# Layer 1 attention with queries and keys in two float32r parts, 34-row packs in both 64-row halves of the array, shared by scores and maximum pass

## Chip, cores and metric

One core of a Trainium2 chip. The metric is the time of one execution of the whole program on the device, in microseconds. The program computes two transformer layers over 2 x 1,024 tokens of width 128; the change lies in the attention of layer 1.

## What is computed

Layer 1's attention, cut to its core (16 heads of width 8, S = 1,024, scores softmaxed without a causal mask, with a decay that depends on the distance of two tokens):

```python
q = x @ W_q
latent_kv = (x @ W_k + x @ W_v) @ W_down_kv          # 32 wide
k_rec = (latent_kv @ W_up_k).reshape(b, s, H, HD).transpose(0, 2, 1, 3)
v_rec = (latent_kv @ W_up_v).reshape(b, s, H, HD).transpose(0, 2, 1, 3)
scores = einsum('bhqd,bhkd->bhqk', qh, k_rec) / sqrt(d) * exp(-0.01 * abs(t[:, None] - t[None, :]))
attn = softmax(scores, axis=-1)
out = einsum('bhqk,bhkd->bhqd', attn, v_rec)
x = layernorm(x + out.reshape(b, s, d) @ W_o)
```

Before it stand layer 0's attention and experts, behind it a normalisation, layer 1's experts and the last layer norm.

## The kernel before

The decay is a product of a growing and a falling exponential on either side of the diagonal, so queries and keys exist in two variants ("var" 0 and 1). `project_l1` works through four groups of 512 tokens. PE multiplies by the weights in float32, VectorE multiplies the result by a decay (line 1011, 4 products a group: two variants of q and of k), ScalarE rounds to bfloat16 (first part), VectorE subtracts (1016), ScalarE rounds again (second part, 967), POOL (two of the last on VectorE, 1001) forms the third part. Parts are stored to DRAM (`q_parts`, `k_parts`). The values, with a column of ones per head, are made by PE at line 928 and copied to `a_V` by VectorE (996).

`attention_l1` works in 8 turns of 4 heads (`NIT`), each in two halves of 512 queries (`NHALF` = 16). A half has 9 groups (`NT`), 144 in all. A group is one key block against 512 queries, in four units, one a head; where the diagonal cuts it, a unit has two matmuls, one for each variant. Group g on PE: scores of three units into a ring of three banks (1317: 74 rows, nine products of parts and two rows that carry minus the query's maximum), then the maximum pass for a later half (1286), the fourth unit, then the weighing of group g-2 (`weigh`, 1336: four heads side by side in four column strips, two passes each). ScalarE takes the exponential of each unit (1373), POOL clears the wrong side of the diagonal in some groups (1260), ScalarE copies a finished half from OUT (1363).

The maximum pass makes for each of 128 queries and one head all 1,024 scores from bfloat16 packs of their own (`MaxPacks`, tiles QM and KM, 32 rows, four row strips of the array) into two slots `mring`; VectorE multiplies by a correction and reduces (1385, one instruction a tile). There are 16 tiles a half, 256 in all; `LEAD` = 22 run before the first group, `issued(g)` says how many are due by group g (one or two a group). When the 16 tiles of a half are read, VectorE negates the maxima and splits them, PE turns them (`turn`, 1295), VectorE copies them (1406), and SP writes them as rows 72 and 73 of the query pack (`max_rows`, 1205).

Each engine runs its program in the order in which it is written. SP's queue carries the pack loads (QP 1180, KP 1192, QM 1084, KM 1094 and 1097), the stores of the outputs, and in halves 1 to 3 the stores of the second batch's parts. Packs are double-buffered by turn. PE waits for them at `scores` with T = 0 and at `max_tile` with i = 0.

## Time and profile before

| | us |
|---|---|
| median of 3 runs | 1570.79 (1562.11 to 1572.23) |
| the profiled execution | 1561.7 |
| its span, first to last instruction | 1559.6 |
| busy: PE, VectorE, ScalarE, POOL | 1334.3, 1128.4, 906.1, 474.1 |
| PE loading weights | 751.4 |
| mean granted clock of TensorE | 0.917 |

Engines: PE is TensorE (PEld its weight loads, which overlap matmuls), DVE VectorE, ACT ScalarE, POOL GpSimd, SP the DMA queue. A duration of a matmul in the rows includes its way through the array, so that neighbours overlap: how far their starts lie apart is the time that one costs. A row with "x3" merges three neighbours, its duration runs from the first start to the last end. PEclk is the granted clock, 1.00 for 2.4 GHz and 0.50 for 1.2. Names in rows leave out digits: `a_QP` is `a1_QP0` or `a1_QP1`.

### The profile page before, as it was taken

The numbers are of one execution on the slowest core, as the hardware profiler recorded it, in microseconds if no ns is written. First come the engines' busy times: TensorE is split into PE (matmuls) and PEld (weight loads), VectorE is DVE, ScalarE is ACT, GpSimd is POOL, SyncE is SP. The second block draws the span as 40 slices with busy tenths as digits, with TensorE's granted clock in tenths as the row PEclk, the third lists the DMA queues.
The fourth block names the chain that finished last, engine by engine and source line by source line (L and its number), as shares of the span: only waits on it lengthen the run. The fifth ranks groups of instructions, "written<-read, shape, count | busy, mean of one in ns | idle before, by whom it ended". The sixth has DMA issues, their size and how long they took to land. (4 is left out here: it accounts for less than half of the span.)

```text
span 1559.6 us, 23543 instructions
## 1 busy us (share of the span) xinstructions
PE 1334.3 (86%) x7952; PEld 751.4 (48%) x7952; DVE 1128.4 (72%) x1737; ACT 906.1 (58%) x1496; POOL 474.1 (30%) x986
## 2 busy tenths in 40 slices
PE   4298988619999999999754989999999979999998
PEld 1133333407877778777321222222222225777776
DVE  4366674377999999998547766888888243778885
ACT  3288885105555555555330766787887802767774
POOL 3255453003343343343220233223442301212210
PEclk8599999859999999999855898999999968999999
DMA  5524420015666666663347556665563040022110
GB/s 139 107 56 88 80 61 8 3 41 127 151 150 147 151 155 140 157 148 72 123 96 92 72 128 123 102 106 87 88 98 49 15 157 3 26 97 82 61 49 27
DMA packets 71415, 142.57 MB, mean 91 GB/s; under 512 B 11815, under 2 KB 44648, under 8 KB 64392
## 3 DMA queue, kind: packets, MB, share of 16 engines
q1 hardware_dynamic: 70660, 140.62, 41.3%
q8 instruction: 59, 0.97, 0.3%
q10 hardware_dynamic: 648, 0.59, 0.1%
q14 instruction: 48, 0.39, 0.1%
HBM read 124.20 MB, written 16.71 MB: 90 GB/s over the span
## 5 line engine op out<-in xcount | busy, mean ns | idle before, releaser
L1385 DVE CUSTOM_DVE_ANT_0 a_junk<-a_mring,a_COR 128x1024 bf16<-128x1024 f32 x256 | 304.8, 1222 | 90.0 <-PE a_mring L1286 89.8
L1373 ACT ACTIVATE a_PR<-a_ring 128x512 f32<-128x512 f32 x576 | 300.7, 603 | 118.7 <-PE a_ring L1317 118.6
L1260 POOL TENSOR_SCALAR_AFFINE_SELECT a_PR<-a_PR 128x128 f32<-128x128 f32 x512 | 134.6, 293 | 304.0 <-ACT a_PR L1373 303.8
L803 ACT ACTIVATE e_HH<-e_H 128x512 fp32r<-128x512 f32 x184 | 116.4, 633 | 162.5 <-DVE e_H L851 161.8
L1317 PE MATMUL a_ring<-a_QP,a_KP 74*128 74x512 bf16 (+3 forms) x768 | 181.2, 341 | 13.1 <-issue 5.7
L402 DVE TENSOR_SCALAR a_PR<-a_PR,a_lo,a_hi 128x1024 f32<-128x1024 f32 (+1 forms) x160 | 122.1, 774 | 77.1 <-ACT a_PR L376 74.4
L376 ACT ACTIVATE a_PR<-a_ring,a_ng 128x1024 f32<-128x1024 f32 (+1 forms) x160 | 155.0, 1033 | 13.3 <-PE a_ring L305 12.5
L1336 PE MATMUL a_OUT<-a_PR,a_V 128*9 128x512 f32 (+3 forms) x1536 | 154.7, 500 | 0.0
L822 DVE TENSOR_TENSOR e_HL<-e_H,e_HH 128x512 fp32r<-128x512 f32 x138 | 140.3, 1017 | 13.2
L1317 PEld LDWEIGHTS a_ring<-a_QP,a_KP 74*128 74x128 bf16 x768 | 57.9, 99 | 172.4 <-ACT a_PR L1373 119.6
L1676 DVE TENSOR_TENSOR e_HL<-e_GL,e_HH 128x512 fp32r<-128x512 f32 x144 | 109.2, 763 | 37.6 <-ACT e_HH L1644 34.1
L745 POOL TENSOR_TENSOR e_HL<-e_H,e_HH 128x512 fp32r<-128x512 f32 x46 | 78.8, 1712 | 181.1 <-ACT e_HH L803 181.1
L278 POOL TENSOR_SCALAR_AFFINE_SELECT a_PR<-a_PR 128x128 f32<-128x128 f32 x256 | 98.5, 410 | 110.6 <-DVE a_PR L402 110.6
L1637 ACT ACTIVATE e_GL<-e_psF,e_BF 128x512 f32<-128x512 f32 x144 | 99.2, 690 | 53.4 <-PE e_psF L1595 52.9
L851 DVE TENSOR_TENSOR e_H<-e_T,e_ROUTE 128x512 f32<-128x512 f32 x176 | 122.9, 698 | 1.5
L845 DVE TENSOR_TENSOR e_T<-e_SG,e_psU 128x512 f32<-128x512 f32 x176 | 119.4, 679 | 1.3 <-PE e_psU L761 1.1
L796 ACT ACTIVATE e_SG<-e_psG 128x512 f32<-128x512 f32 x184 | 108.6, 590 | 17.2 <-PE e_psG L761 17.0
L1286 PE MATMUL a_mring<-a_KM,a_QM 32*128 32x512 bf16 (+3 forms) x704 | 82.9, 349 | 36.0 <-DVE a_top L1385 21.9
L325 PE MATMUL a_OUT<-a_PR,a_V 128*32 128x256 f32 (+1 forms) x1280 | 87.5, 367 | 10.3 <-DVE OALL L407 10.3
L305 PE MATMUL a_ring<-a_QP,a_KP 128*128 128x512 bf16 (+3 forms) x384 | 88.3, 333 | 8.4 <-ACT a_PR L376 8.4
L759 PE MATMUL e_psG<-e_XH,e_WH 128*128 128x512 f32 x184 | 72.5, 394 | 8.6 <-POOL e_WL L740 8.6
L770 PE MATMUL e_acc<-e_HH,e_WH 128*128 128x512 f32 x184 | 76.5, 416 | 3.0 <-POOL e_HL L745 2.8
(232 smaller groups left out, 2344.8 us busy)
## 6 DMA issues: line engine op xcount, KB each, us to landing
e_ROUTE<-routing SPq DMA_DIRECT2D x24, 704.0 KB
a_QP<-q_parts SPq DMA_DIRECT2D x72, 192.0 KB
e_RAW<-in_w_chunks SPq DMA_DIRECT2D x46, 192.0 KB, 7.5
a_QM<-q_parts SPq DMA_DIRECT2D x64, 128.0 KB, 5.4
e_GATE<-gates SPq DMA_DIRECT2D x8, 1024.0 KB, 4.7
e_ROUTE<-routing SPq DMA_DIRECT2D x8, 640.0 KB
a_KP<-k_parts SPq DMA_DIRECT2D x24, 192.0 KB
e_ROUTE<-routing SPq DMA_DIRECT2D x8, 576.0 KB
```

The costliest lines, as they stand in the source:

```text
L376: nc.scalar.activation(PR[T][:, j, 0:WIDTH0[T]], ring[n % RING][:, 0:WIDTH0[T]], ACT.Exp, scale=ng[:, head]).then_inc(ring_read, 1)
L402: nc.vector.tensor_scalar(p, p, lo[:, head], hi[:, head], ALU.max, ALU.min).then_inc(clamped, 1)
L803: nc.scalar.activation(HH[n % NH][:], HT[n % NH][:], ACT.Copy).then_inc(high_done, 1)
L822: nc.vector.tensor_tensor(HL[n % NH][:], HT[n % NH][:], HH[n % NH][:].bitcast(F32), ALU.subtract)\
L845: nc.vector.tensor_tensor(T[n % 2][:], SG[n % 2][:], psU[n % 2][:], ALU.mult).then_inc(mul_done, 1)
L851: nc.vector.tensor_tensor(HT[n % NH][:], T[n % 2][:], ROUTE[c % NW][:, grp(g)], ALU.mult).then_inc(h_ready, 1)
L1260: last = nc.gpsimd.affine_select(out=d, in_=d, compare_op=keep, fill=0.0, base=0, pattern=[[step, P]], channel_multiplier=-step)
L1317: last = nc.tensor.matmul(ring[n % NRING][:, a - h % 2 * GW:b - h % 2 * GW], KP[s][:, j, var, kb * P:(kb + 1) * P], QP[s][:, h % 2, j, var ...
L1336: last = nc.tensor.matmul(OUT[j * HP:j * HP + VC, a:b], V[:, b0 + kb, v0:v0 + VC], PR[g % NPR][:, j, a:b], start=(T == 0), stop=(T == NT - ...
L1373: nc.scalar.activation(PR[g % NPR][:, j, :], ring[n % NRING][:], ACT.Exp).then_inc(s_read, 1)
L1385: nc.vector.tensor_tensor_reduce(out=junk[:, i % 2, :], in0=mring[k % 2][:], in1=COR[:, c:c + S], scale=1.0, scalar=-3.0e38, op0=ALU.mult, ...
L1676: nc.vector.tensor_tensor(HL[n % NH][:], GL[n % 4][:], HH[n % NH][:].bitcast(F32), ALU.subtract).then_inc(low_done, 1)
```

## The change

Queries and keys are kept in two float32r parts instead of three bfloat16 ones. ScalarE rounds once, VectorE subtracts straight into the second part. A pack has 34 rows: four products of parts (32) and the two maximum rows. Heads 0 and 1 of a turn lie in partitions 0 to 33, heads 2 and 3 in 64 to 97. The same packs serve the maximum pass; while it reads a pack, the two rows of the queries must be zero, so POOL clears them (`clear`) and the maxima are written afterwards. The maximum order alternates between the halves of the array (2, 0, 3, 1), and PE alternates pieces of scores in one half with pieces of a maximum tile in the other (`group`). The value products move from the projection to the start of `attention_l1`, their copies to ScalarE. Between the leading maximum tiles stand matmuls whose results nothing uses (`keep_busy`). Stores of heads 4 to 15 of the first batch are issued by ScalarE, those of the second batch in halves 1 to 4 by SP.

The core of the diff follows; of the lines taken away only a few stand, since the functions before are printed above.

```diff
+PARTS1 = 2
...
+        W, parts, first_stored = t["W"], packs.parts, t["first_stored"]
+        DEC = t["PR"][:, 0:2].rearrange("p r j c -> p (r j c)").rearrange("p (w n) -> p w n", w=NV)
+        lat = t["PR"][0:DL + 1, 2].rearrange("p j c -> p (j c)")
+        loaded, dec_loaded = t["loaded"], t["dec_loaded"]
+        kv = sb("p1_kv", [P, TOK], F32)
+        val = sb("p1_val", [P, NV, 2, GW], F32)
...
+                            packs.store(sp, g, w, i, 0, HQ, first_stored)
                 sp.wait_ge(first_stored, 2 * NV * 2 * 16)
...
+                packs.load_q(sp, 0)
+                packs.load_q(sp, 1)
...
+                def high(g, w):
                     act.wait_ge(val_done, g * NV + w + 1)
...
+                    nc.scalar.activation(parts[:, w, 0, grp(g)], val[:, w, g % 2], ACT.Copy).then_inc(high_done, 1)
...
+                act.wait_ge(first_stored, 2 * NV * 2 * 16)
+                packs.load_k(act, 0)
...
+                            dve.wait_ge(high_done, g * NV + w)
+                            nc.vector.tensor_tensor(parts[:, w - 1, 1, grp(g)], val[:, w - 1, g % 2], parts[:, w - 1, 0, grp(g)].bitcast(F32),
+                                                    ALU.subtract).then_inc(low_done, 1)
...
+                nc.gpsimd.memset(lat[DL:DL + 1, :], 1.0).then_inc(rows_set, 1)
+                pool.wait_ge(rows_set, 1)
+                n = 1
+                for h in range(2):
+                    packs.clear(h, rows_set)
+                    pool.wait_ge(rows_set, n + 2)
+                    packs.set_ones(h, rows_set)
+                    pool.wait_ge(rows_set, n + 4)
+                    n += 4
...
-MAX_ORDER = (0, 2, 1, 3)
+HROWS = 64
+NROWS = 2 * PARTS1 * HD
+MAX_ORDER = (2, 0, 3, 1)
...
+class Packs:
+    Q_LOADS, K_LOADS = 2 * 2 * 16, 2 * 3 * 16
     def __init__(self, nc, ctx, QS, KS):
         sb, sem = sbuf(nc, ctx), Sems(nc, ctx)
...
+        self.nc, self.QS, self.KS = nc, QS, KS
+        self.parts = sb("p1_parts", [P, 4, PARTS1, TOK], F32R)
+        self.Q = [sb(f"a1_QP{s}", [HROWS + NROWS + 2, 2, 2, 2, GW], F32R) for s in range(2)]
+        self.K = [sb(f"a1_KP{s}", [HROWS + NROWS + 2, 2, 2, S], F32R) for s in range(2)]
+        self.q_loaded = [[sem(f"q_loaded{s}{half}") for half in range(2)] for s in range(2)]
+        self.k_loaded = [sem(f"k_loaded{s}") for s in range(2)]
+    def store(self, eng, g, w, i, h0, h1, done):
+        tok = slice(g * GW, (g + 1) * GW)
+        eng.dma_start((self.QS if w < 2 else self.KS)[h0:h1, w % 2, i, :, tok], self.parts[h0 * HD:h1 * HD, w, i, tok].bitcast(F32))\
+            .then_inc(done, 16)
+    def load_q(self, eng, h):
+        it, half = h // 2, h % 2
         b, q, s = it // NQUAD, it % NQUAD, it % 2
...
+        tok = slice(b * S + half * GW, b * S + (half + 1) * GW)
+        for pair in range(2):
+            heads = slice(q * HQ + pair * 2, q * HQ + pair * 2 + 2)
             for r in range(2):
...
+                rows = slice(pair * HROWS + r * 16, pair * HROWS + r * 16 + 16)
+                eng.dma_start(self.Q[s][rows, half].rearrange("r h a t -> r (h a) t").bitcast(F32),
+                              self.QS[heads, :, :, :, tok].rearrange("h a i d t -> (i d) (h a) t")).then_inc(self.q_loaded[s][half], 16)
     def load_k(self, eng, it):
         b, q, s = it // NQUAD, it % NQUAD, it % 2
...
+        tok = slice(b * S, (b + 1) * S)
+        for pair in range(2):
+            heads = slice(q * HQ + pair * 2, q * HQ + pair * 2 + 2)
+            r0 = pair * HROWS
+            for rows, i0, i1 in ((slice(r0, r0 + 16), 0, 2), (slice(r0 + 16, r0 + 24), 1, 2), (slice(r0 + 24, r0 + 32), 0, 1)):
+                eng.dma_start(self.K[s][rows].rearrange("r h a t -> r (h a) t").bitcast(F32),
+                              self.KS[heads, :, i0:i1, :, tok].rearrange("h a i d t -> (i d) (h a) t")).then_inc(self.k_loaded[s], 16)
+    def clear(self, h, done):
+        for pair in range(2):
+            rows = slice(pair * HROWS + NROWS, pair * HROWS + NROWS + 2)
+            self.nc.gpsimd.memset(self.Q[h // 2 % 2][rows, h % 2].rearrange("r h a t -> r (h a t)").bitcast(F32), 0.0).then_inc(done, 1)
...
+    def max_head(m):
+        return MAX_ORDER[m % HQ]
+    def unit_head(g, n):
+        first = issued(g - 1) if g else LEAD
+        swap = first < issued(g) and max_head(first) < 2
+        return (2, 3, 0, 1)[n] if swap else n
...
+                    sp.dma_start(OD[h // 2, :, h % 2 * GW:(h % 2 + 1) * GW], OST[h % 2][:]).then_inc(out_stored[h % 2], 16)
                 max_rows(0)
...
+                sp.wait_ge(stored[0], STORES * 16)
+                packs.load_q(sp, 2)
+                packs.load_k(sp, 1)
+                packs.load_q(sp, 3)
                 for h in range(NHALF):
                     it = h // 2
+                    if h % 2 == 0 and 1 <= it < NIT - 1:
+                        sp.wait_ge(s_read, h * UNITS)
+                        packs.load_k(sp, it + 1)
+                        packs.load_q(sp, h + 3)
+                    if h % 2 == 1 and it + 2 < NIT:
+                        sp.wait_ge(s_read, h * UNITS)
+                        if it + 2 == NQUAD:
+                            sp.wait_ge(stored[1], STORES * 16)
+                        packs.load_q(sp, h + 3)
                     if h:
                         store(h - 1)
...
+                    if h + 1 < NHALF:
                         max_rows(h + 1)
...
+                    if LATE_FROM <= h < LATE_FROM + STORES // LATE_EACH:
+                        for n in range((h - LATE_FROM) * LATE_EACH, (h - LATE_FROM + 1) * LATE_EACH):
+                            packs.store(sp, 2 + n // 8, n % 4, n // 4 % 2, 0, H, stored[1])
...
+                def clear(h):
+                    packs.clear(h, cleared)
+                    pool.wait_ge(cleared, (h - 1) * 2)
+                for h in (2, 3):
+                    clear(h)
                 for g in range(NGROUP):
...
+                    T, h = g % NT, g // NT
+                    half = h % 2
+                    if 1 <= h < NHALF - 3 and T == (1 if half else KB // 2 + 1):
+                        pool.wait_ge(s_read, h * UNITS)
+                        pool.wait_ge(masked, masked_groups(g - 1) * HQ)
+                        clear(h + 3)
...
+                    s, row, j = h // 2 % 2, i // HQ, max_head(m)
+                    rows = slice(j // 2 * HROWS, j // 2 * HROWS + NROWS + 2)
+                    if a == 0:
+                        if i == 0:
+                            pe.wait_ge(packs.q_loaded[s][h % 2], (h // 4 + 1) * packs.Q_LOADS)
+                            pe.wait_ge(packs.k_loaded[s], (h // 4 + 1) * packs.K_LOADS)
+                            if h >= 2:
+                                pe.wait_ge(cleared, (h - 1) * 2)
+                        slot_free(k)
+                    last = nc.tensor.matmul(mring[k % 2][:, a:b], QP[s][rows, h % 2, j % 2, var, row * P:(row + 1) * P],
+                                            KP[s][rows, j % 2, var, a:b], start=True, stop=True)
+                    if b == S:
+                        last.then_inc(m_filled, 1)
+                def score_piece(g, n, a, b, kb, var):
+                    h, T, u, j = g // NT, g % NT, g * HQ + n, unit_head(g, n)
+                    s, a, b = h // 2 % 2, a - h % 2 * GW, b - h % 2 * GW
+                    rows = slice(j // 2 * HROWS, j // 2 * HROWS + NROWS + 2)
+                    if a == 0:
+                        if T == 0 and n == 0:
+                            pe.wait_ge(m_rows, (h + 1) * 64)
+                        if u >= NRING:
+                            pe.wait_ge(s_read, u - NRING + 1)
+                    last = nc.tensor.matmul(ring[u % NRING][:, a:b], KP[s][rows, j % 2, var, kb * P:(kb + 1) * P],
+                                            QP[s][rows, h % 2, j % 2, var, a:b], start=True, stop=True)
+                    if b == GW:
+                        last.then_inc(s_filled, 1)
                 def turn(h):
                     k = turn_slots[h]
                     pe.wait_ge(neg_done, 3 * (h + 1))
                     slot_free(k)
                     for part in range(2):
...
+                        last = nc.tensor.transpose(mring[k % 2][0:2 * NTILE, part * GW:part * GW + P], neg_part[:, part, :].bitcast(F32),
+                                                   consts["ident"][:])
                     last.then_inc(m_filled, 1)
...
+                def group(g):
                     for h in range(1, NHALF):
                         if turn_group(h) == g:
                             turn(h)
...
+                    tiles = range(issued(g - 1) if g else LEAD, issued(g))
+                    parts_of_unit = list(segments(g % NT, g // NT % 2))
+                    for two in range(2):
+                        scores = [(n, *piece) for n in (2 * two, 2 * two + 1) for piece in parts_of_unit]
+                        maxima = max_pieces(tiles[two]) if two < len(tiles) else []
+                        for x in range(max(len(scores), len(maxima))):
+                            if x < len(scores):
+                                score_piece(g, *scores[x])
+                            if x < len(maxima):
+                                max_piece(tiles[two], *maxima[x])
...
+                def values(f):
+                    if f >= NRING:
+                        pe.wait_ge(v_kept, f - NRING + 1)
+                    for n in range(f * FILL, min(f * FILL + FILL, B * KB)):
+                        last = nc.tensor.matmul(ring[f % NRING][:, n % FILL * VW:(n % FILL + 1) * VW], lat[:, n * P:(n + 1) * P], WV[:],
+                                                start=True, stop=True)
+                    last.then_inc(v_ready, 1)
+                def keep_busy(n):
+                    nc.tensor.matmul(ring[n % NRING][:], ID[:], ID[:].unsqueeze(1).to_broadcast([P, GW // P, P]), start=True, stop=True)
+                for f in range(NFILL):
+                    values(f)
                 pe.wait_ge(cor_loaded, 32)
...
                 for m in range(LEAD):
                     if m == tiles_until_turn(0):
                         turn(0)
...
+                    for piece in max_pieces(m):
+                        max_piece(m, *piece)
+                    if m == 0:
+                        pe.wait_ge(v_kept, NFILL)
+                    for n in range(2):
+                        keep_busy(n)
+                for n in range(12):
+                    keep_busy(n)
+                pe.wait_ge(out_clear, 1)
                 for g in range(NGROUP + LAG):
                     if g < NGROUP:
...
+                        group(g)
...
+                for f in range(NFILL):
+                    keep_values(f)
+                for n in range(STORES):
+                    packs.store(act, n // 8, n % 4, n // 4 % 2, HQ, H, stored[0])
```

PE in the main loop, one group of an odd half with two maximum tiles. Before, from one weighing (`a_OUT`) to the next, scores in `a_ring`, maxima in `a_mring`:

```order
2403 L1336 MATMUL a_OUT<-a_PR,a_V 9x512 x4
2404 L1317 MATMUL a_ring<-a_QP,a_KP 128x512 x3
2405 L1286 MATMUL a_mring<-a_KM,a_QM 128x384
2406 L1286 MATMUL a_mring<-a_KM,a_QM 128x128
2407 L1286 MATMUL a_mring<-a_KM,a_QM 128x512
2408 L1286 MATMUL a_mring<-a_KM,a_QM 128x384
2409 L1286 MATMUL a_mring<-a_KM,a_QM 128x128
2410 L1286 MATMUL a_mring<-a_KM,a_QM 128x512
2411 L1317 MATMUL a_ring<-a_QP,a_KP 128x512
```

After, a group of the same kind, scores and maxima by turns:

```order
2497 L1302 MATMUL a_OUT<-a_PR,a_V 9x512 x4
2498 L1259 MATMUL a_ring<-a_QP,a_KP 128x512
2499 L1244 MATMUL a_mring<-a_KP,a_QP 128x384
2500 L1259 MATMUL a_ring<-a_QP,a_KP 128x512
2501 L1244 MATMUL a_mring<-a_KP,a_QP 128x128
2502 L1244 MATMUL a_mring<-a_KP,a_QP 128x512
2503 L1259 MATMUL a_ring<-a_QP,a_KP 128x512
2504 L1244 MATMUL a_mring<-a_KP,a_QP 128x384
2505 L1259 MATMUL a_ring<-a_QP,a_KP 128x512
2506 L1244 MATMUL a_mring<-a_KP,a_QP 128x128
2507 L1244 MATMUL a_mring<-a_KP,a_QP 128x512
```

Three scores, maxima, one score have become pairs in which a score's matmul and a maximum's stand side by side. The group that holds the turn, after:

```order
2548 L1302 MATMUL a_OUT<-a_PR,a_V 9x512 x4
2549 L1269 MATMUL a_mring<-ident,a_neg_part 32x128 x2
2550 L1259 MATMUL a_ring<-a_QP,a_KP 128x256
2551 L1244 MATMUL a_mring<-a_KP,a_QP 128x512
2552 L1259 MATMUL a_ring<-a_QP,a_KP 128x256
2553 L1244 MATMUL a_mring<-a_KP,a_QP 128x128
```

Before, the turn (L1295) stood behind three units of scores; now it is ahead of all, and the first maximum piece follows one score piece. SP's queue after, from the start of a turn to the next one's first loads (`q_parts` and `k_parts` to packs, `a_MT` the maximum rows):

```order
299 L1051 DMA a_KP<-k_parts 16x4x1024
300 L1051 DMA a_KP<-k_parts 8x4x1024 x2
301 L1051 DMA a_KP<-k_parts 16x4x1024
302 L1051 DMA a_KP<-k_parts 8x4x1024 x2
303 L1040 DMA a_QP<-q_parts 16x4x512 x4
304 L1163 DMA o_sums<-a_OST 128x512
305 L1157 DMA a_QP<-a_MT 1x16x128 x4
306 L1040 DMA a_QP<-q_parts 16x4x512 x4
```

Before, a turn had six loads of QP, five of KP, eight of QM and twelve of KM; now it has eight of QP and six of KP.

## Rows read from the trace of the kernel before

**Rows 1.** Windows by stage: range, length, busy us (instructions), clock, DMA share, GB/s.
```profile
759.00:814.00 55.00, 34.42 (x72) 14.65 (x72) 28.60 (x42) 22.84 (x40) 19.70 (x15) 0.67 0.37 86
814.00:826.00 12.00, 0.00 (x0) 0.00 (x0) 0.53 (x2) 1.28 (x1) 0.00 (x0) 0.50 0.79 89
826.00:852.00 26.00, 12.54 (x64) 2.71 (x64) 24.18 (x45) 0.00 (x0) 0.00 (x0) 0.50 0.76 99
852.00:870.00 18.00, 18.00 (x106) 5.22 (x104) 12.55 (x22) 11.18 (x22) 8.45 (x32) 0.59 0.08 22
904.00:911.00 7.00, 1.36 (x3) 0.28 (x3) 0.00 (x0) 0.74 (x2) 0.37 (x2) 0.75 0.76 229
960.00:968.00 8.00, 5.92 (x37) 1.75 (x38) 2.38 (x4) 3.22 (x7) 1.55 (x6) 0.64 0.24 72
1043.00:1210.00 167.00, 160.55 (x1338) 47.70 (x1334) 137.95 (x253) 134.78 (x259) 61.41 (x234) 1.00 0.51 83
```

**Rows 2.** Groups by line: operation and count | busy us, mean ns | idle before, releaser.
```profile
L1385 DVE CUSTOM_DVE_ANT_0 a_junk<-a_mring,a_COR 128x1024 bf16<-128x1024 f32 x256 | 304.8, 1222 | 90.0 <-PE a_mring L1286 89.8
L1286 PE MATMUL a_mring<-a_KM,a_QM 32*128 32x512 bf16 (+3 forms) x704 | 82.9, 349 | 36.0 <-DVE a_top L1385 21.9 <-DMA a_KP<-in_ones 12.9
```

**Rows 3.** Timeline of PE, one group of the loop: start, duration, instructions.
```profile
1083.28 0.82 PE L1317 MATMUL a_ring<-a_QP,a_KP 74*128 74x512 bf16 x3
1084.03 0.39 PE L1286 MATMUL a_mring<-a_KM,a_QM 32*128 32x256 bf16 x3
1084.36 0.39 PE L1317 MATMUL a_ring<-a_QP,a_KP 74*128 74x512 bf16 x1
1084.68 1.04 PE L1336 MATMUL a_OUT<-a_PR,a_V 128*9 128x512 f32 x8
1085.65 0.60 PE L1317 MATMUL a_ring<-a_QP,a_KP 74*128 74x512 bf16 x2
```

**Rows 4.** Timeline of PE, the group that holds the turn.
```profile
1077.05 0.82 PE L1317 MATMUL a_ring<-a_QP,a_KP 74*128 74x512 bf16 x3
...
1078.79 0.58 PE L1286 MATMUL a_mring<-a_KM,a_QM 32*128 32x128 bf16 x6 [0.70 <-DVE a_top L1385]
...
1080.60 0.60 PE L1317 MATMUL a_ring<-a_QP,a_KP 74*128 74x512 bf16 x2
```

**Rows 5.** Timeline of ScalarE, copies of finished halves out of OUT.
```profile
885.31 0.60 ACT L1363 ACTIVATE a_OST<-a_OUT 128x512 f32<-128x512 f32 x1 [0.41 <-PE a_OUT L1336]
...
1043.23 0.60 ACT L1363 ACTIVATE a_OST<-a_OUT 128x512 f32<-128x512 f32 x1 [0.41 <-PE a_OUT L1336]
...
1067.15 0.60 ACT L1363 ACTIVATE a_OST<-a_OUT 128x512 f32<-128x512 f32 x1 [0.41 <-PE a_OUT L1336]
...
1232.47 0.60 ACT L1363 ACTIVATE a_OST<-a_OUT 128x512 f32<-128x512 f32 x1
...
1251.05 0.60 ACT L1363 ACTIVATE a_OST<-a_OUT 128x512 f32<-128x512 f32 x1 [1.75 <-PE a_OUT L1336]
```

**Rows 6.** Float32r matmuls of layer 0's experts, and weight loads by type.
```profile
600.40 0.39 PE L761 MATMUL e_psG<-e_XH,e_WL 128*128 128x512 f32 x1
600.63 0.39 PE L759 MATMUL e_psU<-e_XH,e_WH 128*128 128x512 f32 x1
...
L761 PEld LDWEIGHTS e_psG<-e_XH,e_WL 128*128 128x128 f32 x184 | 34.8, 189 | 7.5
L1317 PEld LDWEIGHTS a_ring<-a_QP,a_KP 74*128 74x128 bf16 x768 | 57.9, 99 | 172.4 <-ACT a_PR L1373 119.6 <-issue 33.6 <-DMA a_KP<-k_parts 3.4
...
751.80 0.97 PEld L496 LDWEIGHTS n0m_scale<-mean_of,n0m_Q 128*128 128x128 f32 x8 [0.26 <-ACT n0m_Q L533]
```

**Rows 7.** The projection: VectorE's product, and PE's passes in order of time.
```profile
L1011 DVE TENSOR_TENSOR p_val<-p_psQ,p_DEC 128x512 f32<-128x512 f32 x8 | 5.1, 678 | 3.5 <-PE p_psQ L920 3.5
...
760.10 1.02 PE L917 MATMUL p_psKV<-X,p_wv 128*128 128x512 f32 x2
760.96 1.02 PE L920 MATMUL p_psQ<-X,p_wq 128*128 128x512 f32 x2
```

297 lines of the change are left out of this document (65 added, 232 removed).

## The prediction

> **What bounds the kernel now.** The change touches one stretch, layer 1's projection and attention, so I read the windows by stage first. The projection takes 759 to 814 us, then come 12 us in which no compute engine does anything, 26 us in which only the maximum pass runs ahead, and the main loop from 852 to 1251 [rows 1]. In the undisturbed part (1043 to 1210, the last row) PE is busy 160.6 of 167 us at full clock, VectorE 138.0, ScalarE 134.8. The reader should see that PE sets the pace there and that the next two bounds lie close together.
>
> The copies out of OUT mark the halves: 1043.23 to 1067.15 is 23.9 us per half of nine groups, 2.66 us a group; the last one, which has no maxima beside it, takes 18.6 (1232.47 to 1251.05) [rows 5]. Scaled to one half, VectorE is busy 23.9 x 138.0/167 = 19.7 us and ScalarE 23.9 x 134.8/167 = 19.3: however fast PE becomes, a half with maxima costs about 19.7.
>
> Inside one group [rows 3] PE does: three scores from 1083.28, maxima at 1084.03, one score at 1084.36, the weighing at 1084.68, next group at 1085.65, in all 2.37 us. Two scores stand 0.215 apart ((0.82 - 0.39)/2), so three end their streams at 1083.93, yet the maxima start 0.10 later; the same 0.10 stands at each of the four changes between the 74-row, 32-row and 9-column shapes. The sum is 4 x 0.215 + 0.23 (maxima, in four row strips at once) + 0.87 (weighing: 0.97 less one gap) + 4 x 0.10 = 2.36. A second tile in a group adds 0.3. That is where the change works. The Trainium skill (TensorEngine Tiling, Key Properties) says that a change of tiling mode drains the engine; the trace agrees with 0.10 us.
>
> **Part 1, the loop on PE.** Removed: two of four shape changes a group (-0.20), and the maxima's own slot (-0.23, or -0.5 with two tiles), since a maximum tile runs in the 64-row half that the scores do not use. Each half of the array then has 1,024 columns per pair of scores, 2,048 a group. In float32r a 512-column matmul steps at 0.23 (600.40 to 600.63), scores and pairs 4 x 0.2275 = 0.91 [rows 6].
>
> Added: the weight loads. A float32r load lasts 189 ns where the 74-row bf16 one lasts 99, and eight float32 loads in a row take 0.97, (0.97 - 0.19)/7 = 0.111 each [rows 6]. Each of 768 + 704 = 1,472 pieces has one: 10.2 a group, 1.13 us if one port serves both halves, which is more than the 0.91 of streaming. Two bounds for one group, PE in program order (the ten pieces of the two-tile group whose rows stand above: 512/384/512/128/512, then the same with the halves of the array swapped), a load allowed once the piece before it in its half has started:
> - one port for both halves: starts at 0.11, 0.22, 0.34, 0.44, 0.56, 0.78, 0.78, 1.01, 1.01, 1.12, end 1.35;
> - a port each: 0.11, 0.11, 0.34, 0.34, 0.45, 0.68, 0.68, 0.90, 0.90, 1.02, end 1.24.
>
> Worked through in the same way, the groups of the loop average 1.39 and 1.15: split scores cost most with one port (14 loads), and a long score holds the short maximum piece behind it. With 0.87 weighing and 2 x 0.09 for changes: 2.43 or 2.20 a group, 21.9 or 19.8 a half. Then the turn: before, it and VectorE's lateness (0.70 idle) made its group 3.55 us long, 1077.05 to 1080.60, 0.9 over the mean [rows 4]. Now it stands ahead of the group's scores, in float32, and only one score lies between it and a maximum piece that waits for VectorE. Behind that piece all other scores are queued and ScalarE waits for them. I take 1.2. A half is 23.1 or 21.0; I take the middle, 22.0, because no row shows two 64-row float32r loads side by side. Tiles are issued through 131 groups, 14.6 halves: 14.6 x (23.9 - 22.0) = **28 us** less; bounds +12 (23.1) and +61 (19.7, VectorE).
>
> The Trainium skill (TensorE: Matmul & The Clock Gate, Weight-path perf modes) keeps fast weight load for types other than FP32; that speaks against this change. The 189 against 99 ns agree. If it were only that, with own ports, the sum keeps 2.20 a group; by one port 2.43.
>
> **Part 2, the projection, 55 us** [rows 1]. Gone: the second rounding on ScalarE, the third part on POOL, the value products and their copies, the reuse waits on POOL. Per group of 512 tokens VectorE keeps 4 products at 0.68 and 4 subtractions, which I put at 0.8 because POOL clears rows beside them (0.68 to 1.0): 6.0 us. PE has ten passes of 0.43 (760.10 to 760.96 is two) = 4.3 [rows 7], so VectorE leads: 4 x 6.0 + 3 to start + 1 = 29, **26 us** less. If PE stays at the low clock (0.67 mean before), 8.6 a group, 37 in all: 18 less.
>
> **Part 3, to the first maximum, 12 us.** Before, PE waited 12.9 for DMAs queued with packs [rows 2]. After, ScalarE issues the first K pack (1 MB) behind its last rounding, six DMAs. At the 89 to 229 GB/s of [rows 1] it lands in 5 to 11 us; the value products (six copies at 0.6) lie beside that. I take 6 from the end of the projection: **6 us** less, bounds 0 to 8.
>
> **Part 4, the lead, 26 us.** VectorE sets it, 22 tiles. The filler matmuls make PE need 0.62 (one tile in one half, with loads) + 2 x 0.215 + 0.2 changes = 1.25 a tile where VectorE steps at 304.8/256 = 1.19 [rows 2]: +1.5. At low clock the first three or so take a microsecond more: +3. Twelve fillers of 0.215 behind the last tile, 2.6 us beside VectorE's last two (2.4), then PE's own first scores: +0.5. **5 us** more. In return the loop starts warm: the first copy-out at 885.3 comes 33.2 after 852 where eleven groups at 2.66 take 29.2, so **4 us** less.
>
> **Part 5, pack loads.** PE stood still in 904 to 911 (busy 1.4 of 7) and lost time again in 960 to 968 [rows 1]. The loop lasts 1251 - 852 = 399 us, where 14.6 halves at 23.9, 1.4 at 18.6 and two groups of lag at 2.4 make 380; 4 of the 19 are the cold start, 15 lie here. By the shapes of their DMAs the packs shrink from 31 MB to 17, and one pair of packs is left of two. But K of the next turn can load only when the turn before last is read, and its first maximum tile is due 5.6 groups later, 13 us; 1 MB needs 5 to 11 by the rates above. It fits, except where late stores (1 MB a half in halves 1 to 4) share the queue. I take 4 of the 15 as left: **11 us** less. ScalarE's 16 early stores (3.1 MB) lie beside the lead, 25 us; they would delay the second K pack if they took longer.
>
> POOL's clears stand in groups without masks; SP's four row DMAs instead of two fit into the 2.4 groups before they are due. Both at nothing; without that cover 1 to 2 us a half, in the range.
>
> **Sum.** 28 + 26 + 6 - 5 + 4 + 11 = 70. The profiled execution took 1561.7 (span 1559.6), so 1492. The median of the three runs is 1570.8, 9 above it; I move the forecast by 3 of those to **1495**.
>
> **Rivals.**
> - *VectorE is the bound at once* (own ports, turn hidden): 19.7 to 20.5 a half, 50 to 61 in the loop, 1459 to 1470. For it: 138 of 167 us busy. Against: the turn. 0.20.
> - *A load waits for its own half.* Load and stream then add: 0.11 + 0.23 twice for scores, 3 x 0.11 + 0.455 = 0.79 for three pieces, two pairs 1.58, + 1.05 = 2.63 a group: before's pace, 1523. Rows against: full-array float32r loads of 189 ns hide behind a 0.23 step. The Trainium skill (TensorE: Matmul & The Clock Gate, What overlaps and what doesn't) lets a load overlap only in another row group, which is this rival. 0.10.
> - *The halves do not run together.* (2,048 + 1,820) columns at 0.2275/512 = 1.72, + 1.05 = 2.77 a group, 25 a half, +16 instead of -28: 1536. Against: before, 1,024 columns of maxima pass in 0.23. 0.12.
> - *Slower than before*: a float32r load in a 64-row half waits until the array is empty and nothing streams beside it. Loads and streams of both halves then add up: 1.72 + 1.13 + 1.05 = 3.9 a group, 35 a half, +163 - 42: about 1680. Against: before, bf16 loads lie beside other strips' matmuls, and float32r ones of the full array hide. The other parts save 42, so it decides from 23.9 + 42/14.6 = 26.8 a half, 2.97 a group. 0.05.
> - The forecast, 1475 to 1512: 0.53.
>
> What is wanted is a sign beyond about 1%, what a measurement of this kernel can tell from no change. Faster 0.92, same 0.03, slower 0.05. The range, 1458 to 1538, takes in the first two rivals and half of the third and leaves some 0.12 outside.
>
> **What would show it.** A half near 22.0 between copies out, PE over 90% busy and VectorE near 19.7/22; 23 or more says one port. The gap between a maximum piece and the score beside it tells whether halves overlap. The projection near 29 at clock above 0.9. No idle of PE on K packs in turns 2 and 3. If the turn's group costs over 2 us more than its neighbours, the held-back scores were underestimated; if PE waits for K in every turn, part 5 falls.

## The result and the profile after

The changed kernel takes 1764.8 us (median of 4 runs, 1761.05 to 1780.65), beside 1566.8 for the kernel before on the same chip. The ratio is 1.128, with a 95% interval of 1.120 to 1.137: it is 198 us slower. The profiled execution has a span of 1759.1 us against 1559.6, and a mean granted clock of 0.771 against 0.917. A time below that stands without a range is that of one execution. One of the 24 executions of the kernel before that were timed beside these kernels took 1659.12 us, at a mean granted clock of 0.784, and enters none of the ratios.

The page of the kernel after comes first: busy time by engine, the rows of PE and of the granted clock over the span, and the costliest groups of the attention.

```profile
PE 1575.9 (90%) x7977; PEld 911.2 (52%) x8008; DVE 1127.6 (64%) x1727; ACT 902.0 (51%) x1486; POOL 527.9 (30%) x1008
...
PE   3488987199999999868999999999999988999998
...
PEclk8699998599999999985555555556655555899999
...
L1377 DVE CUSTOM_DVE_ANT_0 a_junk<-a_mring,a_COR 128x1024 bf16<-128x1024 f32 x256 | 307.6, 1223 | 268.7 <-PE a_mring L1244 268.4
L1365 ACT ACTIVATE a_PR<-a_ring 128x512 f32<-128x512 f32 x576 | 302.0, 598 | 300.8 <-PE a_ring L1259 299.3
L1259 PE MATMUL a_ring<-a_QP,a_KP 34*128 34x512 f32 (+3 forms) x768 | 319.0, 574 | 3.9 <-ACT a_PR L1365 3.8
L1259 PEld LDWEIGHTS a_ring<-a_QP,a_KP 34*128 34x128 f32 x768 | 187.0, 299 | 245.0 <-issue 181.0
```

VectorE's reduction and ScalarE's exponentials take as long each as before (the reduction 1223 ns, 1222 in [rows 2]), and then wait for PE, 268 and 300 us. PE itself shows hardly any idle time. What has changed is the row PEclk: a slice of the span is 44 us, and most of those of this attention have the digit 5, half of the full clock. The page shows no stall. Whoever reads only the busy shares sees a PE that is at its limit.

The windows by stage, which answer to [rows 1], with the same columns (projection; to the first maximum; the lead; then the main loop in five pieces):

```profile
760.00:791.00 31.00, 20.34 (x40) 6.24 (x40) 20.11 (x32) 13.77 (x24) 23.00 (x9) 0.86 0.35 68
791.00:805.35 14.35, 8.02 (x33) 7.73 (x33) 0.48 (x1) 2.89 (x6) 7.19 (x4) 0.50 0.74 113
805.35:858.15 52.80, 52.80 (x120) 20.90 (x120) 27.97 (x48) 1.28 (x1) 0.00 (x0) 0.51 0.32 73
858.15:864.00 5.85, 4.81 (x36) 3.53 (x37) 5.04 (x9) 5.16 (x10) 3.47 (x14) 1.00 0.90 87
865.00:1215.00 350.00, 350.00 (x1743) 149.11 (x1737) 186.54 (x332) 179.79 (x342) 106.18 (x294) 0.50 0.26 47
1219.00:1242.00 23.00, 21.56 (x202) 10.87 (x200) 18.00 (x30) 18.15 (x36) 14.72 (x53) 0.99 0.55 68
1242.00:1244.00 2.00, 0.91 (x4) 0.61 (x4) 0.88 (x5) 0.58 (x2) 1.95 (x2) 0.80 0.53 76
1244.00:1436.00 192.00, 189.51 (x900) 76.19 (x903) 81.12 (x145) 99.23 (x189) 45.90 (x149) 0.50 0.11 20
```

For 350 us PE is busy 350.0 us and its granted clock is 0.50 of 2.4 GHz, that is 1.2 GHz. Before, the comparable stretch had 1.00 with PE *less* busy, 160.6 of 167 us. The copies out of OUT, which answer to [rows 5], give the price of a half:

```profile
1126.93 0.60 ACT L1347 ACTIVATE a_OST<-a_OUT 128x512 f32<-128x512 f32 x1 [1.48 <-PE a_OUT L1302]
1164.37 0.60 ACT L1347 ACTIVATE a_OST<-a_OUT 128x512 f32<-128x512 f32 x1 [1.26 <-PE a_OUT L1302]
1202.45 0.60 ACT L1347 ACTIVATE a_OST<-a_OUT 128x512 f32<-128x512 f32 x1 [1.48 <-PE a_OUT L1302]
1232.60 0.60 ACT L1347 ACTIVATE a_OST<-a_OUT 128x512 f32<-128x512 f32 x1 [0.17 <-PE a_OUT L1302]
...
1448.81 0.60 ACT L1347 ACTIVATE a_OST<-a_OUT 128x512 f32<-128x512 f32 x1 [4.09 <-PE a_OUT L1302]
```

A half takes 37.4 or 38.1 us where it took 23.9; only the one in which the clock rose, from 1202.45, takes 30.1, and the one in which it fell again, behind it, 35.2. The clock was up for 24 us.

Where the 199.5 us of span come from, stage by stage: from the start of the projection to the first maximum 759 to 826 before, 760 to 805.35 after, 21.7 less; the lead 26 before, 52.8 after, 26.8 more; from the end of the lead to the last copy out 399.1 before (852 to 1251.05 with the start of the copy) and 590.7 after (858.15 to 1448.81), 191.6 more. Together 196.7; nearly all of it is the loop.

### The profile page after: what moved, and what is told of

Read it like the earlier page. It is cut to its first block and busy times, and to the rows that moved or that the text cites. A ratio compares the mean times of both kernels' runs of the same rounds, so it can differ in the third digit from the quotient of the medians.

```text
span 1759.1 us, 23558 instructions
## 1 busy us (share of the span) xinstructions
PE 1575.9 (90%) x7977; PEld 911.2 (52%) x8008; DVE 1127.6 (64%) x1727; ACT 902.0 (51%) x1486; POOL 527.9 (30%) x1008
## 5 line engine op out<-in xcount | busy, mean ns | idle before, releaser
L1377 DVE CUSTOM_DVE_ANT_0 a_junk<-a_mring,a_COR 128x1024 bf16<-128x1024 f32 x256 | 307.6, 1223 | 268.7 <-PE a_mring L1244 268.4
L1259 PE MATMUL a_ring<-a_QP,a_KP 34*128 34x512 f32 (+3 forms) x768 | 319.0, 574 | 3.9 <-ACT a_PR L1365 3.8
L1259 PEld LDWEIGHTS a_ring<-a_QP,a_KP 34*128 34x128 f32 x768 | 187.0, 299 | 245.0 <-issue 181.0
L1244 PE MATMUL a_mring<-a_KP,a_QP 34*128 34x512 f32 (+3 forms) x704 | 294.3, 558 | 8.2 <-DMA a_KP<-k_parts 5.6
L1302 PE MATMUL a_OUT<-a_PR,a_V 128*9 128x512 f32 (+3 forms) x1536 | 265.0, 810 | 0.0
L1244 PEld LDWEIGHTS a_mring<-a_KP,a_QP 34*128 34x128 f32 x704 | 172.9, 303 | 28.6 <-issue 24.8
L1668 DVE TENSOR_TENSOR e_HL<-e_GL,e_HH 128x512 fp32r<-128x512 f32 x144 | 108.1, 755 | 37.1 <-ACT e_HH L1636 33.5
L797 ACT ACTIVATE e_SG<-e_psG 128x512 f32<-128x512 f32 x184 | 108.6, 590 | 16.9 <-PE e_psG L762 16.9
L306 PE MATMUL a_ring<-a_QP,a_KP 128*128 128x512 bf16 (+3 forms) x353 | 80.2, 328 | 11.2 <-ACT a_PR L377 8.3
L1058 POOL MEMSET a_QP<- 2x2048 f32 x32 | 57.5, 1798 | 94.8 <-issue 67.6
```

The costliest lines, as they stand in the source:

```text
L1244: last = nc.tensor.matmul(mring[k % 2][:, a:b], QP[s][rows, h % 2, j % 2, var, row * P:(row + 1) * P], KP[s][rows, j % 2, var, a:b], start ...
L1259: last = nc.tensor.matmul(ring[u % NRING][:, a:b], KP[s][rows, j % 2, var, kb * P:(kb + 1) * P], QP[s][rows, h % 2, j % 2, var, a:b], star ...
L1302: last = nc.tensor.matmul(OUT[j * HP:j * HP + VC, a:b], V[:, b0 + kb, v0:v0 + VC], PR[:, g % NPR, j, a:b], start=(T == 0), stop=(T == NT - ...
L1377: nc.vector.tensor_tensor_reduce(out=junk[:, i % 2, :], in0=mring[k % 2][:], in1=COR[:, c:c + S], scale=1.0, scalar=-3.0e38, op0=ALU.mult, ...
```

## Two things to tell apart: the clock, and the loop at equal clock

The trace of the kernel after has both clocks in it, so one group of the loop can be read at each. First PE's timeline at clock 0.50:

```profile
1200.49 1.89 PE L1302 MATMUL a_OUT<-a_PR,a_V 128*9 128x512 f32 x8
1202.31 0.79 PE L1259 MATMUL a_ring<-a_QP,a_KP 34*128 34x512 f32 x1
1202.31 0.79 PE L1244 MATMUL a_mring<-a_KP,a_QP 34*128 34x384 f32 x2
...
1204.73 1.04 PE L1302 MATMUL a_OUT<-a_PR,a_V 128*9 128x512 f32 x4
```

Then a group in the 23 us at full clock, and ScalarE beside it:

```profile
1226.19 1.05 PE L1302 MATMUL a_OUT<-a_PR,a_V 128*9 128x256 f32 x16
1227.17 0.50 PE L1259 MATMUL a_ring<-a_QP,a_KP 34*128 34x512 f32 x1
1227.18 0.50 PE L1244 MATMUL a_mring<-a_KP,a_QP 34*128 34x512 f32 x1
1227.51 0.39 PE L1259 MATMUL a_ring<-a_QP,a_KP 34*128 34x512 f32 x1
1227.51 0.62 PE L1244 MATMUL a_mring<-a_KP,a_QP 34*128 34x256 f32 x3
1227.75 0.40 PE L1259 MATMUL a_ring<-a_QP,a_KP 34*128 34x512 f32 x1
1228.36 0.49 PE L1259 MATMUL a_ring<-a_QP,a_KP 34*128 34x512 f32 x1 [0.21 <-ACT a_PR L1365]
...
1228.79 0.51 PE L1302 MATMUL a_OUT<-a_PR,a_V 128*9 128x384 f32 x4
...
1227.71 1.57 ACT L1365 ACTIVATE a_PR<-a_ring 128x512 f32<-128x512 f32 x3 [0.53 <-PE a_ring L1259]
```

From weighing to weighing it is 4.24 us at the low clock and 2.60 at the full one. The second number matters as much as the first: the forecast was 2.20 to 2.43. The score and the maximum piece do start together (1227.17 and 1227.18, 1227.51 both), so the two halves of the array run side by side, and each has its own path for weights. But PE then stands still before the fourth score, which waits for ScalarE to free one of the three slots. The group is a round trip, that is a chain in which each engine waits for the other once: the first score starts at 1227.17, ScalarE begins to read it at 1227.71 and has freed the slot for the fourth score at 1228.36, in all 1.19; the weighing follows after 0.43; the next group's first score starts 0.98 behind it (1226.19 to 1227.17). The sum is 2.60, and no term of it is the maximum pass. So there were two theories to settle: what holds the clock down, and what sets the loop once the clock is up.

## The experiments

For the clock, theory R says that what counts is how many rows of the array the pieces fill: 34 in each half after, 74 in the scores before. Theory T says that it is the type, by the slower weight loads or by what float32r does in the array. Four kernels tested them.

**The type undone.** The kernel after with parts and packs in bf16, still 34 rows:

```diff
-        self.Q = [sb(f"a1_QP{s}", [HROWS + NROWS + 2, 2, 2, 2, GW], F32R) for s in range(2)]
-        self.K = [sb(f"a1_KP{s}", [HROWS + NROWS + 2, 2, 2, S], F32R) for s in range(2)]
+        self.Q = [sb(f"a1_QP{s}", [HROWS + NROWS + 2, 2, 2, 2, GW], BF16) for s in range(2)]
+        self.K = [sb(f"a1_KP{s}", [HROWS + NROWS + 2, 2, 2, S], BF16) for s in range(2)]
```

> The changed kernel with its parts, packs and maximum rows in bfloat16 in place of float32r (same 34 rows, same order, same two halves; two bf16 parts, so the scores are coarser). Theory R (rows): the granted clock in the loop follows how many rows of the array the matmuls fill, and 34 are too few whatever the type; then the clock stays at 0.50 in most of the loop, a half between copies out stays near 37.6 us and the whole near 1750. Theory T (type): float32r with its 189 ns loads is what keeps the clock down; then the clock is 1.00 in the loop, a half 23.5 or less and the whole near 1530.

It took 1604.6 us. Halves were 33.5 and 34.5 us at clock 0.50 until about 1039, and then 23.0 and 23.1 at 1.00 until about 1247, just behind the last maxima; from there the clock was 0.50 again, and the last two halves took 27.9 and 28.5. Two windows of that kernel:

```profile
900.00:1000.00 100.00, 100.00 (x589) 25.33 (x589) 60.21 (x108) 57.27 (x111) 39.12 (x127) 0.50 0.18 43
1050.00:1200.00 150.00, 135.41 (x1254) 39.74 (x1251) 129.41 (x236) 125.44 (x243) 80.84 (x234) 1.00 0.17 38
```

So the low clock is not float32r's doing: bf16 has it too, from 856 to 1039 with PE busy 183.0 of 183 us. But the same 34 rows can also run at 1.00, which a plain reading of R does not allow.

**The rows filled.** The kernel after in float32r, each half's pack widened to 64 rows with zeros in rows 34 to 63:

```diff
-                    rows = slice(j // 2 * HROWS, j // 2 * HROWS + NROWS + 2)
+                    rows = slice(j // 2 * HROWS, j // 2 * HROWS + HROWS)
```

> The changed kernel with the contraction widened from 34 to 64 rows in each half; rows 34 to 63 hold zeros in queries and keys, so the sums are the same. POOL has eight more clears at the start of the projection, some 28 us beside it, of which about 10 may show. Theory R: the clock rises to 1.00 in the loop, a half is 23.4 us (the group of 2.59 us that the changed kernel shows at full clock, times nine), the whole near 1570. Theory T: nothing changes, clock 0.50 in the loop, a half 37.6, the whole near 1770. If zeros don't count, R also gives this; so a stay at 0.50 alone would not settle it.

It took 1603.0 us. The clock in the loop is 0.98 and 0.99 in two long windows, with halves of 24.9 us where no K pack is late. The third and fourth line are the time behind the longest wait for a K pack (2.2 us, until 995.93):

```profile
900.00:1000.00 100.00, 91.13 (x741) 41.70 (x741) 78.01 (x142) 74.26 (x144) 48.12 (x136) 0.98 0.46 86
1050.00:1200.00 150.00, 137.18 (x1117) 63.11 (x1118) 117.85 (x212) 111.15 (x216) 69.23 (x200) 0.99 0.35 53
...
995.00:1005.90 10.90, 9.97 (x50) 4.47 (x50) 5.13 (x11) 3.88 (x8) 1.85 (x2) 0.53 0.35 88
1006.00:1015.00 9.00, 8.41 (x61) 3.03 (x59) 7.02 (x13) 6.96 (x14) 3.60 (x2) 1.00 0.48 105
```

Same type, same number and lengths of matmuls, rows of zeros added, 162 us less. That is theory R, and zeros count as rows. With 64 rows the clock falls behind a wait too, but it is back within 11 us.

**The rows taken from the kernel before.** The old kernel with its scores over 34 of their 74 rows:

```diff
-                                                KP[s][:, j, var, kb * P:(kb + 1) * P],
-                                                QP[s][:, h % 2, j, var, a - h % 2 * GW:b - h % 2 * GW],
+                                                KP[s][0:34, j, var, kb * P:(kb + 1) * P],
+                                                QP[s][0:34, h % 2, j, var, a - h % 2 * GW:b - h % 2 * GW],
```

> The kernel before with the scores contracted over rows 0 to 33 of its packs only, in bfloat16; 40 of 74 rows of products and the maximum rows are left out. Order, loads and number of matmuls are the same. Theory R: the granted clock falls to 0.50 in the loop, a half goes from 23.9 to about 38 us and the whole from 1562 to about 1760. Theory T: clock and halves stay, 1562.

It took 1792.2 us, slower than the change itself, with less arithmetic than the kernel before:

```profile
1050.00:1200.00 150.00, 150.00 (x731) 31.20 (x730) 75.06 (x137) 76.87 (x143) 33.95 (x128) 0.50 0.34 55
```

Halves are 39.5 us. One edit of two slices, nothing else of the change, brings a loss as large as that of the change. That leaves theory T nothing to explain of the clock.

**Full-array matmuls as a remedy.** The kernel after with one 128-row bf16 filler, as those in the lead, in each group of the loop:

```diff
+                        if n in (0,):
+                            keep_busy(u)
```

> The changed kernel with one filler matmul a group (128 rows, 512 columns, bf16) ahead of the group's first score, into the ring slot that this score then overwrites. It costs 0.22 us plus up to 0.2 for two more shape changes a group. Theory R: the added full-array stream lifts the clock in the loop, a half is then about 9 x 3.0 = 27 us instead of 37.6 and the whole near 1620; if one is too few, the clock stays and each half is 9 x 0.5 = 4 us longer, 1840. Theory T, that slow loads hold the array: the clock stays at 0.50, 1840.

It took 1695.4 us, halves of 27.4 to 37.5 with a clock of 0.73 on average from 1050 to 1200. One filler a group lifts the clock for parts of a half and costs its own time; it is no remedy.

For the second question, and for what the 34 rows do when the clock is up, seven more kernels followed. Theory L is the round trip read above. Its rival P is that PE's own work sets the group.

**64 rows without the fillers of the lead.**

```diff
-                    for n in range(2):
-                        keep_busy(n)
```

> The kernel after with 64 rows a head (rows 34 to 63 hold zeros), without the two filler matmuls per tile in the lead, and with the clears of the second pair of packs moved from the projection to POOL's start of the attention. Nothing of the computation is left out. Theory R (rows that the packs fill set the granted clock; at 64 rows the loop runs at clock 1.00): halves of 24.9 us as in the run with 64 rows (1603 us). The projection no longer waits for eight clears of about 3.5 us, and in the lead each of 22 tiles loses two fillers that take 0.43 us each at clock 0.50: 1603 - 14 - 19 to 1603 - 28 - 19, so 1556 to 1570. Rival F (the fillers in the lead are what lifts the clock for the loop): the clock stays at 0.50 behind the lead and halves take 37 us for at least a part of the loop, over 1620.

It took 1557.05 us (1552.55 to 1565.17, 9 runs), 0.9936 of the kernel before, 95% interval 0.9914 to 0.9958, so it is 0.6% faster. The clears of the second pair of packs also moved out of the projection. The 46 us below the run with 64 rows are the two savings, those clears and the fillers, together; rival F falls, since the clock is 1.00 from 864 to 960 and 0.98 from there to 1200 without those fillers. The halves are still 24.9 us, or 25.4 to 27.9 with a late K pack. This is the change with its clock repaired: in the profiled run the first half is copied out at 876.3, 9 us before [rows 5], and the last at 1252.69, 1.6 behind them. What projection and lead win, the loop gives back.

**The weighing in two parts.** The next kernel puts 256 columns of the weighing behind each pair of scores, so that PE has work while ScalarE frees a slot:

```diff
                             if x < len(maxima):
                                 max_piece(tiles[two], *maxima[x])
+                        if g >= LAG:
+                            weigh(g - LAG, two)
```

> The kernel before this one in the list, with the weighing of a group cut into two parts of 256 columns, one behind each pair of scores, instead of 512 columns behind all four. Theory L (a cycle of latencies sets the group: ScalarE frees a slot, fourth score, weighing, first score of the next group, ScalarE again; PE's own streams take less): the two parts of 0.44 us stand where PE waited anyway, a half falls from 24.9 us to 21 to 22.5, the whole by 14.6 x 2.4 to 14.6 x 3.9 = 35 to 57 us below the kernel before this one. Rival P (PE's own work, with a change of shape at 0.10 us each, sets the group): there are four more changes or two, a half grows by 9 x 0.2 = 1.8 us to 26.7, the whole by 26 us.

1552.3 us. Halves without a late K pack go from 24.9 to 24.0, those with one take 25.2 to 28.1. P's sign was wrong (it had 26.7), so the wait for a slot was real. But L's 21 to 22.5 was wrong too: only 0.9 of the 2.4 to 3.9 us came. The bf16 form tells why.

> As the one before, with parts, packs and row maxima in bf16 instead of float32r (two bf16 parts, so the scores are less precise). Theory L with dear float32r loads (0.189 against 0.099 us): halves of 20 to 21.5 us at clock 1.00, limited by VectorE's 19.7 us a half, 15 to 25 us in all below the float32r form. Rival T (the type makes no difference once the clock is 1.00): halves equal to those of the float32r form within 0.3 us.

1501.5 us, halves of 21.7 to 22.2, one of 23.7. Between these two kernels only the type differs, and it is worth 2.1 us a half at full clock: in float32r the load that each piece brings stays visible, in bf16 it doesn't. (A piece behind a gap is followed 0.34 us later by the next one in float32r and 0.23 in bf16; that the load makes the difference is read from its price of 0.11 in [rows 6], no run tests it apart from the type.) The same shows without the split, at 34 rows: 23.05 in bf16, 24.6 to 24.9 in float32r (below), 1.7 us. The rival that the type makes no difference at clock 1.00 falls. In both of these kernels the second part of the first weighing sets the start flag again, so 256 columns lose the first key block's summand; work and times are those of the mended form below.

**The fillers of the lead by themselves**, taken out of the kernel after and nothing else:

> The kernel after, only the two filler matmuls per tile in the lead left out (the twelve behind it stay). It prices the fillers by themselves. Theory R: in the lead at clock 0.50 each tile takes 2.1 to 2.2 us with them and about 1.3 without, 22 tiles: 15 to 20 us less in the lead, and the loop runs at clock 0.50 as before, 37 to 38 us a half: 1741 to 1750. Rival F (the fillers hold a clock that would otherwise be lower): the lead gains nothing, or loses.

1705.3 us, 36 less than the lower end of the expectation. The lead gave what was expected (52.8 us in the kernel after, 807.11 to 840.89 now, 19 less; rival F falls again); the rest came from a stretch at full clock that theory R did not foresee. The windows of this kernel:

```profile
864.00:960.00 96.00, 89.12 (x731) 40.87 (x731) 76.78 (x137) 74.03 (x145) 44.83 (x135) 1.00 0.46 86
960.00:964.00 4.00, 2.54 (x22) 1.00 (x22) 2.73 (x7) 1.65 (x4) 3.03 (x2) 0.81 0.41 85
964.00:1200.00 236.00, 236.00 (x1183) 102.23 (x1182) 126.65 (x225) 121.12 (x230) 72.92 (x204) 0.50 0.24 40
```

For 96 us the 34-row loop holds the full clock, in halves of 24.8 to 25.3. Then PE waits for a K pack, and behind that the clock is 0.50 with PE busy 236.0 of 236 us. PE's timeline at that place:

```profile
959.53 0.39 PE L1259 MATMUL a_ring<-a_QP,a_KP 34*128 34x512 f32 x1
961.46 0.29 PE L1244 MATMUL a_mring<-a_KP,a_QP 34*128 34x128 f32 x1 [1.54 <-issue]
...
963.70 0.61 PE L1269 MATMUL a_mring<-ident,a_neg_part 128*32 128x128 f32 x2
```

The kernel after does the same at the end of its 23 us: a score starts at 1240.91, the next piece at 1243.09 behind a wait for K (issued at 1227.2), and from 1244 the clock is 0.50. The next kernel tests that.

**No late K packs**, at 34 rows, by cutting the K loads from the third turn on:

```diff
-        tok = slice(b * S, (b + 1) * S)
+        n = S if it < 2 else S // 16
+        tok = slice(b * S, b * S + n)
```

> The kernel after without the fillers in the lead (float32r, 34 rows), and with the K loads from the third turn on cut to a sixteenth of their columns, so that later turns use keys of other heads and the result differs: it leaves out 15/16 of those loads and nothing of the engines' work. Theory P (PE's pause at a late K pack throws the clock, and 34 rows keep a clock that they already have): no pause, so once at 1.00 the loop stays there, 14 halves of 24.9 us, in all 1540 to 1570. Rival R (34 rows cannot hold the clock for long, pause or not): the clock falls to 0.50 within a few halves and stays there, halves of 37.4 to 38.1, over 1650.

```profile
895.00:935.00 40.00, 40.00 (x231) 20.16 (x227) 20.93 (x37) 21.12 (x40) 18.85 (x62) 0.50 0.19 50
935.00:940.00 5.00, 5.00 (x34) 2.02 (x36) 3.60 (x9) 2.19 (x6) 0.78 (x1) 0.62 0.01 2
940.00:1200.00 260.00, 242.76 (x1986) 110.16 (x1979) 209.63 (x379) 201.49 (x391) 120.26 (x340) 1.00 0.21 46
...
1246.00:1280.00 34.00, 32.39 (x145) 10.20 (x144) 0.00 (x0) 16.46 (x32) 8.54 (x32) 0.50 0.02 8
```

1589.8 us. The loop starts at 0.50 this time (one half of 37.4 us, one of 30.7), comes up at about 938 and then holds 1.00 with no pause in 260 us, halves of 24.6 and 24.9. Theory P of this run (P for pause, not the P above) holds only as long as there are maxima: the clock stays up over 300 us. It falls at about 1246, some 12 us behind the last maximum tile, in groups in which PE stood still for no more than 0.45 us at a time; the last line is what follows, and the last half takes 31.8. The run with 64 rows and no fillers has 1.00 in the same part of its loop (1232 to 1252), with PE busy only 16.9 of 20 us. So pauses aren't the only thing that takes the clock from 34 rows. The total missed 1540 to 1570 by 20 us, since neither how late the clock comes up nor the fall at the end is in the theory.

**The best form, mended, and the same with 34 rows.** Start flag on the first part alone:

```diff
-                                                    PR[:, g % NPR, j, a:b], start=(T == 0), stop=(T == NT - 1), skip_group_check=True)
+                                                    PR[:, g % NPR, j, a:b], start=(T == 0 and two == 0), stop=(T == NT - 1 and two == 1), skip_group_check=True)
```

> The bf16 form with 64 rows, no fillers in the lead and the weighing in two parts, now with the start flag on the first part alone: in the two runs of the split form before, the start flag of group 0 stood on the second part too, which threw away the first group's summand of the first 256 columns. Same instructions and same waits otherwise, so the time is that of the run before, 1501 us, 1495 to 1508; against the kernel before 0.955 to 0.963. Rival (the loss of the summand had shortened something, or the one look was a lucky one): over 1515.

> The bf16 form with the weighing in two parts and no fillers in the lead, but with 34 rows a head as in the kernel after: only the zero rows are taken away from the first kernel of this list. Theory R (the filled rows decide whether the clock comes back after a stretch at 0.50): at least a part of the loop runs at 0.50 with halves over 30 us, 1530 to 1680. Rival (with PE's gaps closed, 34 rows are enough): halves of 21.8 to 22.2 us throughout, within 10 us of the form with 64 rows.

The first took 1497.1 us (1492.1 to 1498.3, 4 runs), 0.955 of the kernel before, 95% interval 0.949 to 0.962. The second took 1680.7, with halves of 27.0 to 36.5 us. The only difference between the two is the zero rows and the clears that they need. The window of the form with 64 rows, then that with 34:

```profile
900.00:1000.00 100.00, 92.50 (x1152) 28.80 (x1145) 90.06 (x168) 91.80 (x171) 53.30 (x148) 1.00 0.20 49
```

```profile
900.00:1000.00 100.00, 98.85 (x698) 22.20 (x696) 58.86 (x100) 55.49 (x103) 31.68 (x74) 0.50 0.15 38
```

With 64 rows PE, VectorE and ScalarE are all busy 90 to 92.5 of 100 us, at 21.7 to 22.2 us a half, but for one of 23.7. With 34 rows they do 61% as much work in the same 100 us. The zero rows cost no matmul time: at clock 1.00 PE gets through 733 matmuls between 864 and 960 with 64 rows in float32r, and 731 with 34. Their price is on POOL: in the float32r form eight clears of 3.5 us, 28 in all, half of them moved out of the projection since. ScalarE's row shows that the round trip is gone:

```profile
1002.64 5.44 ACT L1380 ACTIVATE a_PR<-a_ring 128x512 f32<-128x512 f32 x10
```

Ten exponentials without a gap, 0.54 each, where at full clock the kernel after left 0.53 us in every group. This form uses two bf16 parts where before there were three, so its scores are less exact than those of both kernels.

## Why the prediction was wrong

1495 was predicted, 1458 to 1538, with 0.05 for slower; 1764.8 came. Each term of the sum:

- **The clock, in every term.** The failing step is one that the text took without working: the row of [rows 1] with clock 1.00 was carried over to the new shapes. Part 1 prices every piece at full clock, and the low clock was given to the projection and the lead alone, at 3 us. What the runs showed in its place: 34-row pieces stay at 1.2 GHz with PE busy 350.0 of 350 us. At 37.4 and 38.1 against 22.0 a half, 14.6 x (37.75 - 22.0) = 230, less about 10 for the halves at mixed clock; the last half, without maxima, takes 31.2 instead of 18.6 (1417.58 to 1448.81), 13 more. These are 233 of the 270 us between 1495 and 1765; the lead below has 26, the first maximum 8. The 0.05 for slower was for another mechanism, a load that waits for an empty array, and doesn't count in its favour.
- **Part 1 at equal clock: the step that takes the maxima's own slot and two shape changes off the group.** It failed too. At clock 1.00 a half of 34-row float32r takes 24.75 (the run with cut K loads), not 22.0, and more than the 23.9 of before. The streaming sum of 2.20 to 2.43 was right for what PE does and wrong as a bound, because the loop is a round trip over three slots, and the maxima lay in its shadow already. The trace of the kernel before had it. In [rows 3] the fourth score starts 1.08 after the first, where three streams take 0.65; the weighing follows after 0.32, the next group after 0.97; the sum is 2.37. The same three terms after are 1.19, 0.43 and 0.98. The maxima were no term before either. The last half of the kernel before, which has none, shows it:

```profile
1237.28 0.82 PE L1317 MATMUL a_ring<-a_QP,a_KP 74*128 74x512 bf16 x3
1238.36 0.39 PE L1317 MATMUL a_ring<-a_QP,a_KP 74*128 74x512 bf16 x1 [0.26 <-ACT a_PR L1373]
1238.68 1.05 PE L1336 MATMUL a_OUT<-a_PR,a_V 128*9 128x512 f32 x8
1239.66 0.83 PE L1317 MATMUL a_ring<-a_QP,a_KP 74*128 74x128 bf16 x6
```

  Again 1.08, 0.32 and 0.98, in all 2.38, and PE stands still for ScalarE where the maxima were: in the prediction's sum the 0.23 and the 0.10 on either side of it stood for this wait. So taking their slot away gives nothing, and each of the first two terms has grown by 0.11, the price of one float32r load in [rows 6]: 9 x 0.22 = 2.0 us a half more. The half is only 0.8 longer than 23.9, so about 1.2 came back elsewhere in it; where, was not looked into. PE "busy 160.6 of 167" hid the round trip, because the maxima filled the wait and a matmul's duration includes its way through the array.
- **The halves of the array run together** (rival 3 false), and **loads of the two halves lie side by side**, own ports, right. A load hides behind a stream of its own half except behind a gap or a change, where the step is 0.34 and not 0.24 (1227.17 to 1227.51, then 1227.75), and the type is worth 1.7 to 2.1 us a half at full clock. The Trainium skill (TensorE: Matmul & The Clock Gate, Weight-path perf modes), which speaks against float32 weights here, was right in sign; the runs put the price at about 2 us a half.
- **Part 2, projection 29:** 31, with the gain of 24 for 26. Right in mechanism, with errors that cancel: from the second group on VectorE leads, at 5.2 to 5.5 us a group and not 6.0, but the first group took 10.8 (763.00 to 773.77). PE had the low clock from about 782.
- **Part 3, 6 us to the first maximum:** 14.35. The term was undersized by 8 us. From its issue at 788.40 to the first maximum at 805.35 are 17 us, not 5 to 11. The queues moved 113 GB/s, which is a rate of [rows 1], but the K pack shared it with the stores and loads beside it: 1 MB in 17 us is some 62 GB/s.
- **Part 4, +5 - 4:** +26.8. The price "+3 at low clock" took it that the clock comes up within three tiles; the clock stayed at 0.50 for the whole lead. PE in it, after:

```profile
837.94 1.22 PE L1244 MATMUL a_mring<-a_KP,a_QP 34*128 34x512 f32 x2
839.10 1.03 PE L1317 MATMUL a_ring<-a_ID 128*128 128x512 bf16 x2
840.06 1.33 PE L1244 MATMUL a_mring<-a_KP,a_QP 34*128 34x512 f32 x3
```

  A tile takes 2.12 (837.94 to 840.06), of which two fillers are 0.96. They do not raise the clock. The fourteen in a row at the end do (1.00 from about 857), and the loop loses it by 864.
- **Part 5, 11 us from the packs:** the stall is still there, 2.2 us at 1240.9 and again in the 64-row form, and it does something that the text had not priced: the clock falls behind it.
- **"The halves don't run together" and "a load waits for an empty array"** gave times on the slow side, 1536 and 1680, and neither is what happened. The list of rivals had no case in which the clock changes, though the text named both levels and one of its terms used them. By the rows, such a rival was there to work out: two stretches of [rows 1] have a low clock with PE little busy, one has 0.59 with PE busy 18.00 of 18.00 (852 to 870). With two levels, 0.59 means some 15 of the 18 us at the lower one, so as much busy time had not raised the clock; the row was read only as a cold start.

The Trainium skill (TensorE: Matmul & The Clock Gate, What's actually happening) ties the granted clock to how busy PE has been. This case disagrees in one direction: PE busy 350.0 of 350 us stays at 0.50. It agrees in the other, in part: a pause of 2 us was followed by the fall, but so were stretches in which PE stood still for less than 0.7 us at a time.
